# Edge sum, relu and low part of a graph layer as one 1024-column operation each instead of two of 512

## The reference

```
m = concatenate([h[edge_src], w], axis=1)          # 100000 edges, 256 + 3 features
tmp = relu(m @ W1.T + b1)
h_N = segment_sum(tmp, edge_dst, num_segments=3125) # the edges are sorted by this index
h_lin = relu(concatenate([h, h_N], axis=1) @ W2.T)
gnn = h_lin / max(norm(h_lin), 1e-12)
```

## Time and profile before

| what | value |
|---|---|
| median of 3 runs | 2581.1 us (2573.97 to 2582.83) |
| profiled execution | 2579.73 us |
| its span | 2578.0 us |
| PE busy | 2063.5 us (80%) |
| DVE busy | 1574.6 us (61%) |
| ACT busy | 1028.3 us (40%) |
| POOL busy | 1340.7 us (52%) |
| mean granted TensorE clock | 0.912 of full speed |

### The profile page before, as it was taken

How to read it: one execution, slowest core, us unless ns; L and a number is a source line. 1 busy time by engine, 2 the same in 40 slices (tenths; PEclk the granted TensorE clock), 3 DMA queues, 4 the chain that set the end, 5 groups by cost and what they waited for, 6 DMA issues and landing times. The chain is left out here.

```text
span 2578.0 us, 38507 instructions
## 1 busy us (share of the span) xinstructions
PE 2063.5 (80%) x10686; PEld 1658.4 (64%) x10686; DVE 1574.6 (61%) x3709; ACT 1028.3 (40%) x2338; POOL 1340.7 (52%) x1224
## 2 busy tenths in 40 slices
PE   1438799998879999987999997889999674799930
PEld 1326677776667777766777776667777563799920
DVE  4637777776777777677777767767776456211126
ACT  1214444444434444353544444444444232233310
POOL 3135566666556666655666665556666300332245
PEclk9759999999989999999999999999999786799965
DMA  5532222224222222232222223222222221799943
GB/s 154 182 91 59 64 69 68 68 68 105 63 65 70 67 67 67 72 99 68 66 66 67 67 70 102 58 63 66 68 68 68 74 70 50 243 334 327 323 134 95
DMA packets 261053, 260.75 MB, mean 101 GB/s; under 512 B 148507, under 2 KB 193426, under 8 KB 260942
## 3 DMA queue, kind: packets, MB, share of 16 engines
q0 software_dynamic: 124672, 132.82, 21.0%
q1 hardware_dynamic: 132158, 126.66, 15.4%
q10 hardware_dynamic: 4112, 0.03, 0.1%
HBM read 229.85 MB, written 28.39 MB: 100 GB/s over the span
## 5 line engine op out<-in xcount | busy, mean ns | idle before, releaser
L426 POOL DMA_INDIRECT G<-P_d,stage x896 | 1150.5, 1284 | 749.5 <-DVE z L405 459.7
L373 ACT ACTIVATE zr<-z 125x512 fp32r<-125x512 f32 x448 | 274.8, 638 | 524.4 <-DVE z L405 363.1
L405 DVE TENSOR_TENSOR z<-bank,G 125x512 f32<-125x512 f32 x448 | 293.2, 686 | 282.4 <-PE bank L365 125.8
L1152 PE MATMUL bank<-TT,W_s 128*128 128x250 f32 (+1 forms) x1280 | 374.0, 444 | 5.7 <-ACT TT L810 5.1
L1023 PE MATMUL bank<-W_s,hid 128*125 128x256 f32 x1600 | 359.6, 379 | 0.0
L1023 PEld LDWEIGHTS bank<-W_s,hid 128*125 128x125 f32 x1600 | 292.8, 188 | 42.7
L1152 PEld LDWEIGHTS bank<-TT,W_s 128*128 128x128 f32 x1280 | 243.6, 197 | 110.7 <-ACT TT L810 14.9
L379 DVE SCALAR_TENSOR_TENSOR zl<-z,zr 125x512 fp32r<-125x512 f32 x448 | 288.3, 684 | 39.9 <-ACT zr L373 39.9
L357 PE MATMUL bank<-zr,onehot 125*125 125x256 f32 x896 | 271.1, 334 | 12.4 <-DVE zl L379 12.4
L1017 PE MATMUL bank<-ident,hn 125*128 125x125 f32 x700 | 138.2, 306 | 139.7 <-DVE hn L1360 61.6
L358 PE MATMUL bank<-zl,onehot 125*125 125x256 f32 x896 | 230.1, 287 | 0.0
(11 more groups left out here) (283 smaller groups left out, 3058.1 us busy)
## 6 DMA issues: line engine op xcount, KB each, us to landing
W_s<-in_L_ffn_w SPq DMA_DIRECT2D x64, 512.0 KB
hid<-in_L_ffn_w SPq DMA_DIRECT2D x64, 512.0 KB
G<-P_d,stage POOLq DMA_INDIRECT x896
W_s<-in_L_mix_W SPq DMA_DIRECT2D x8, 1024.0 KB
aT<-attr_d SPq DMA_DIRECT2D x224, 31.2 KB
slot_out<-yo SPq DMA_DIRECT2D x32, 128.0 KB
slot_out<-eT SPq DMA_DIRECT2D x32, 128.0 KB
X<-in_x SPq DMA_DIRECT2D x5, 625.0 KB
```

Of the source, the lines that this page charges most:

```text
L373: nc.scalar.activation(zr[:, s, k, :], z[:, k, :], ACT.Relu).then_inc(r_done, 1)
L405: nc.vector.tensor_tensor(z[:, k, :], edge_bank[k][0:ET, :], G[:, ST * s + 2 * k:ST * s + 2 * k + 2, :].rearrange("p j d -> p (j d)"), ALU ...
L426: nc.gpsimd.indirect_dma_start(G[:, j, :], None, P_d[:, :], bass.IndirectOffsetOnAxis(ap=stage[s][:, j:j + 1], axis=0)).then_inc(g_in[j], 16)
L1152: ins = pe.matmul(to[:, 0:(b - a) * T], W1_s[:, k, part], TT[:, k, TT_PIECES[pc]], start=k == 0, stop=k == KD - 1)
```

## The change

Banks 1 and 2 become one PSUM tensor `edge_pair` of 1024 columns, with `bank[1]` and `bank[2]` as its halves. The two PE matmuls stay as they are. The sum z, the relu and the low part are each one operation on 1024 columns. Each semaphore still rises by 2 per pair, but in one step when the whole operation is done, and each operation waits for both halves of what it reads.

```diff
-        bank = [pb(f"bank{i}", [128, 512]) for i in range(8)]
+        bank = [pb("bank0", [128, 512])]
+        edge_pair = pb("edge_pair", [128, 2 * 512])
+        bank += [edge_pair[:, 0:512], edge_pair[:, 512:1024]]
+        bank += [pb(f"bank{i}", [128, 512]) for i in range(3, 8)]
...
         def act_edges(ge, s):
-            for k in range(2):
-                nc.scalar.wait_ge(z_done, ge * 2 + (k + 5))
-                nc.scalar.activation(zr[:, s, k, :], z[:, k, :], ACT.Relu).then_inc(r_done, 1)
+            flat = lambda t: t.rearrange("p k n -> p (k n)")
+            nc.scalar.wait_ge(z_done, ge * 2 + 6)
+            nc.scalar.activation(flat(zr[:, s, :, :]), flat(z[:, :, :]), ACT.Relu).then_inc(r_done, 2)
 
         def dve_low(ge, s):
-            for k in range(2):
-                nc.vector.wait_ge(r_done, ge * 2 + (k + 1))
-                nc.vector.scalar_tensor_tensor(zl[:, k, :], z[:, k, :], 0.0, zr[:, s, k, :].bitcast(f32), ALU.max, ALU.subtract).then_inc(lo_done, 1)
+            flat = lambda t: t.rearrange("p k n -> p (k n)")
+            nc.vector.wait_ge(r_done, ge * 2 + 2)
+            nc.vector.scalar_tensor_tensor(flat(zl[:, :, :]), flat(z[:, :, :]), 0.0, flat(zr[:, s, :, :]).bitcast(f32), ALU.max, ALU.subtract).then_inc(lo_done, 2)
...
             nc.vector.wait_ge(lo_done, ge * 2 + 2)
-            for k in range(2):
-                nc.vector.wait_ge(e_done, ge * 2 + (k + 1))
-                for j in (ST * s + 2 * k, ST * s + 2 * k + 1):
-                    nc.vector.wait_ge(g_in[j], group * 16 + 16)
-                nc.vector.tensor_tensor(z[:, k, :], edge_bank[k][0:ET, :],
-                                        G[:, ST * s + 2 * k:ST * s + 2 * k + 2, :].rearrange("p j d -> p (j d)"),
-                                        ALU.add).then_inc(z_done, 1)
+            nc.vector.wait_ge(e_done, ge * 2 + 2)
+            for j in range(ST * s, ST * s + ST):
+                nc.vector.wait_ge(g_in[j], group * 16 + 16)
+            nc.vector.tensor_tensor(z[:, :, :].rearrange("p k n -> p (k n)"), edge_pair[0:ET, :],
+                                    G[:, ST * s:ST * s + ST, :].rearrange("p j d -> p (j d)"), ALU.add).then_inc(z_done, 2)
```

## The result

The changed kernel takes **2698.7 us** (median of 4 runs, 2697.97 to 2699.74) against 2581.4 of the kernel before in the same job. The ratio is 1.0461, 95% interval [1.044, 1.0481]: slower by 117 us. Forecast were 2648 and 2612 to 2674, so the sign was right and the size outside the range. The profiled execution's span grew from 2578.0 to 2697.4 us, by 119.4.

The account below looks back on a forecast made before the run. PE was taken as nearly the bound, lengthened by waits on DVE, ACT and POOL. Layers at 16.5 us (last 14.0) sum to 63.5; with start 2.1 and end 2.4, 68 on 2579.7 gives 2648 us, range 2612 to 2674.

Parts of the forecast that it names:

- The prices: Merged operations on 1024 columns: z and `zl` 1.22 us each, the relu 1.06; z's upper bound was 1.37.
- Phase one: Loops between a layer's five phase-one groups: each grows by 1.42 us through DVE's serial chain, 5.7 us a layer.
- the handovers: Passing from z to relu and from relu to `zl` between DVE and ACT: 0.04 us each.
- Start: Before the layers, PE waits for hn, which stands on DVE behind four pairs paced by gathers: +2.1 us.
- ends with middle: End of phase one and middle: later gathers and pair delay the queries, 2.2 us a layer, plus 0.4 for copies.
- Phase two, first four groups: Later gather restart, z and relu delay the GELU PE waits for: 1.5 us a group, 5.4 a layer.
- The slack assumed in one group of four: Phase two groups where PE did not wait for the GELU: slack goes first, so 0.9 us instead of 1.5.
- The last groups and the end: PE waits for the whole `zl` and later gathers: +2.5 us at a layer's last group, +2.4 at the kernel's end.
- the head: Start of the next layer: it absorbs most of its own pairs' loss, leaving a guessed 0.3 us a layer.
- the clock: Rival, chance 0.13: more PE idling adds ten slow-clock stretches, 14 to 30 us more, giving 2662 to 2678 us.
- Phase two hides it: Rival, chance 0.2: GELU slack and POOL's pauses absorb the later z in phase two, giving 2619 to 2626 us.
- the operation count pays: Rival, chance 0.03: DVE's occupied time bounds a stage, each pair gains 0.14 us, 31 in all, giving 2549 us.

Follow-up runs that it names:

- e3: The kernel before with only the low part `zl` as one operation on 1024 columns, z and relu in halves: 2631.4 us, ratio 1.0202.
- e4: The changed kernel with only the low part `zl` back in two operations of 512 columns: 2684.1 us, ratio 1.0403 against the kernel before.
- e5: The kernel before with POOL's gathers restarting only when both halves of z are done, all operations still halves: 2612.1 us, ratio 1.0128.
- e8: The kernel before with the first half of z waiting for everything the whole z waits for, operations still halves: 2613.9 us, ratio 1.0132.
- e11: The changed kernel with PE's idle time filled by transposing the next group's first tile nine times: 2690.3 us, ratio 1.0437 against the kernel before.
- e2: The kernel before with only z as one operation on 1024 columns, relu and `zl` in halves: 2654.4 us, ratio 1.0297.
- e1: The kernel before with only the relu as one operation on 1024 columns, z and `zl` in halves: 2639.5 us, ratio 1.0233.
- e7: The kernel before with the one-hot moved ahead of `zl` on DVE: 2608.2 us, ratio 1.0108.
- e10: The kernel before with ACT's relu of step 4 in phase two moved behind the GELUs of f = 7: 2566.2 us, ratio 0.9954.

## Why the prediction was right and wrong

- **The prices held**, to 0.01 us, with the price of reading across two banks, 1.220 us, at its lower bound.
- **Phase one held:** 1.62 us a loop for 1.42. The rest is the handovers, 0.10 each and not 0.04. Start (2.2 for 2.1) held, and ends with middle came 2.9 us under.
- **The step that failed is "Phase two, first four groups", mis-sized:** 5.4 us a layer, measured 14.4. Its mechanism (gathers restart later, z, relu and GELU come later, PE waits) is what the rows show, but its terms lacked two things. First, "POOL then issues without a pause to step 4" took POOL's instructions at their old length. They are stretched beside a whole `zl` and the one-hot: in the group shown z of step 4 came 1.48 us later after the group's start than before, of which 0.54 is the release and 0.95 the stretching. With the longer z and relu PE's wait ends 2.49 us later, where the sum had 1.49. e3 and e4 go the same way (1.19 us a group added, 1.05 given back), though they hold more than the stretching. Second, the sum took PE's work behind a wait at its old length. It runs partly at the lower clock: 0.88 us on the 20 query products of that group, 0.91 in the mean of the 16, and 0.94 on all of PE's work in a group. e5 and e8 show it without any long operation: the two waits together were in the sum for about 1.06 us a group and cost 1.55 and 1.30 alone. The slack assumed in one group of four was not there either: PE waits for the GELU in all 16.
- **The last groups and the end** failed with the same step. Their 2.5 held only the later release and the later `zl`, not the stretched gathers: 6.8 us measured for 2.8 with the head, and 5.9 for 2.4. The 6.8 also hold the next layer's first phase-one group, whose two pairs the sum put at the head's 0.3. Which of the two weighs more was not tried.
- **The rival "the clock"** had the mechanism and a price of 14 to 30 us. In the query products alone it is 19 us of PE's busy time (109.8 to 128.9), and in e11 they were busy for 115.6. By the mean granted clock, 0.912 before and 0.904 after, what was withheld of full speed went from about 227 to 259 us over the whole span, so the clock can be at most some 32 of the 119.4. It was held for unlikely because PE would idle "by 1 to 2 us more, not by many". PE's wait for the GELU went from 12.4 / 16 = 0.8 to 49.9 / 16 = 3.1 us a group, and all 16 groups then had slow products, where 3 had them before. But the lower level was no newcomer: 14 of the 16 groups before had a stretch of it, 58 us together, and the 16 after have 82. As a rival it had been set against the forecast; it comes on top.
- **"Phase two hides it"** fell, as PE's waits had said, and so did **"the operation count pays"**. DVE's busy time fell by 27 us (1574.6 to 1547.4), 31 forecast, and it bought nothing. The Trainium skill's page "VectorE: DVE Perf Modes", section "Rules for kernel authors", asks for fewer operations; here the measurement decides against it: every stage of the table became longer.

What stays open: how the 3.6 us of a group divide among the three operations. z alone is the largest (2.72 in e2, without any added stretching). The parts alone (0.68, 2.72 and 1.19) add up to 4.59, so they share something. What makes the clock fall in one group and not in the next is open too.

## What to carry to other kernels

Before merging two halves of a chain over several engines, look for the wait that the halves hide (here 39.9 us grew to 202.9), and go by when the last half is finished, not by the number of instructions. Where an engine's queue of gathers is on the path, ask which operation of VectorE with two SBUF inputs lies beside them and for how long. And price an idle time of TensorE with what follows it at the lower clock as well, as a range, for not every wait brings it; a wait in front of ready work, like the GELU behind the relu, is the cheap thing to move, but by one place only after a look at what stands next.

## What the hardware showed that I had not expected

- An index copy of 0.20 us on GpSimd took 0.96 us beside a 1.23 us `zl`; the stretched part of GpSimd's instructions went from 60.7 to 107.2 us with half as many, twice as long `zl`.
- With z and relu whole, halves of `zl`, 0.68 us each and back to back, stretched it far less than one of 1.22 (67.6 us against 107.2); but halves in other places, in e1 and e7, came to 82 and 84.
- Of the instructions of GpSimd that started beside VectorE's `zl` or one-hot, both inputs in SBUF, 204 of 210 were stretched; of the 95 that started beside z, one input in PSUM, none.
- In e10 TensorE idled for longer in a group than in the kernel before (3.94 us for 3.42) and had the higher clock (1.00 in 13 groups of 16, for two).
- With the same instructions, a phase-one loop took 21.2 us at a granted clock of 1.00 and 22.8 at 0.93, by turns in one execution.
- A gather of 64 rows costs GpSimd 0.92 us and one of 125 rows 1.21, so about half of its time does not go with the rows (an estimate by a line through the two: 0.62 us).
